# Two-way stage: the next batch's rows turned between two convolution products, and a batch's outputs behind the third

## The reference, cut to what matters

```python
residual = x
xn = layer_norm(x, ln_g, ln_b)
proj = xn @ Wi + bi
xg, z = (proj[..., :D], proj[..., D:])
f = conv1d_same(xg, Wf_conv, bf_conv)
f = simple_ssm(f, af, bf, cf, df)
b_in = jnp.flip(xg, axis=1)
bb_out = conv1d_same(b_in, Wb_conv, bb_conv)
bb_out = simple_ssm(bb_out, ab, bb, cb, db)
bb_out = jnp.flip(bb_out, axis=1)
zg = jax.nn.silu(z)
y = f * zg + bb_out * zg
return y @ Wo + bo + residual
```

## Time and profile before

| | us |
|---|---|
| median of 3 runs | 2517.73 (2516.26 to 2517.88) |
| the profiled execution, its own time | 2510.39 |
| its span, first to last instruction | 2508.4 |
| two-way stage, from GpSimd's first clearing of `xA` to the last addition of outputs | 1757.70 to 1939.76 |
| TensorE busy in the span | 2218.3 (88%) |
| VectorE busy in the span | 1376.1 (55%) |
| ScalarE busy in the span | 1142.9 (46%) |
| GpSimd busy in the span | 879.5 (35%) |
| mean granted TensorE clock, 1 is full speed | 0.948 |

### The profile page before, as it was taken

How to read it: one execution, slowest core, us unless ns; L and a number is a source line. 1 busy time by engine, 2 the same in 40 slices (tenths; PEclk the granted TensorE clock), 3 DMA queues, 4 the chain that set the end, 5 groups by cost and what they waited for, 6 DMA issues and landing times. The chain is left out here.

```text
span 2508.4 us, 45795 instructions
## 1 busy us (share of the span) xinstructions
PE 2218.3 (88%) x16643; PEld 2035.3 (81%) x16643; DVE 1376.1 (55%) x3656; ACT 1142.9 (46%) x2203; POOL 879.5 (35%) x769
## 2 busy tenths in 40 slices
PE   2999999999999999999999885949697889978988
PEld 1999999899899899899899885949355566668988
DVE  4666667567567567567567552412576355532222
ACT  1655665555555555555555441312333455533320
POOL 4445555554554554554554531111321000000000
PEclk9999999999999999999999897979899899988989
DMA  5600000000000000000000202555000010108966
GB/s 167 214 4 4 4 4 5 7 6 4 7 5 4 9 4 4 9 4 4 9 4 2 62 1 76 175 168 157 19 14 5 25 50 38 50 37 274 330 215 220
DMA packets 101337, 150.66 MB, mean 60 GB/s; under 512 B 14692, under 2 KB 79118, under 8 KB 100364
## 3 DMA queue, kind: packets, MB, share of 16 engines
q1 hardware_dynamic: 77580, 118.36, 14.9%
q10 hardware_dynamic: 17984, 20.30, 2.5%
q0 software_dynamic: 5568, 9.27, 1.2%
HBM read 102.32 MB, written 45.50 MB: 59 GB/s over the span
## 5 line engine op out<-in xcount | busy, mean ns | idle before, releaser
L292 PE MATMUL banks<-t_wt,t_l 128*128 128x128 f32 x8508 | 1058.2, 279 | 4.1 <-ACT t_l L369 2.9
L292 PEld LDWEIGHTS banks<-t_wt,t_l 128*128 128x128 f32 x8508 | 1027.6, 195 | 18.9 <-ACT t_l L369 3.7
L468 POOL TENSOR_TENSOR t_rstd<-t_var,t_minus_half 128x4 f32<-128x4 f32 (+1 forms) x379 | 367.0, 968 | 690.6 <-DVE t_var L397 690.4
L351 ACT ACTIVATE t_sq<-banks 128x512 f32<-128x512 f32 (+1 forms) x379 | 216.0, 570 | 530.9 <-PE banks L292 529.3
L405 DVE TENSOR_TENSOR t_yn<-banks,t_rstd 128x512 f32<-128x512 f32 (+1 forms) x379 | 249.2, 657 | 348.3 <-POOL t_rstd L468 341.9
L385 ACT ACTIVATE t_l<-banks,t_cols 128x512 f32<-128x512 f32 x376 | 286.8, 778 | 121.1 <-PE banks L341 117.7
L394 DVE TENSOR_REDUCE t_ss<-t_sq 128x4 f32<-128x512 f32 (+1 forms) x379 | 245.3, 647 | 151.2 <-ACT t_sq L351 142.3
L474 POOL TENSOR_TENSOR t_zrstd<-t_zvar,t_minus_half 128x8 f32<-128x8 f32 x188 | 307.7, 1637 | 25.4 <-DVE t_zvar L432 25.4
L369 ACT ACTIVATE t_l<-banks,t_cols 128x512 f32<-128x512 f32 (+1 forms) x381 | 285.1, 748 | 16.5 <-PE banks L301 11.7
L301 PE MATMUL banks<-t_ident,t_yn 128*128 128x128 f32 x1426 | 219.4, 273 | 17.1 <-DVE t_yn L405 15.8
L301 PEld LDWEIGHTS banks<-t_ident,t_yn 128*128 128x128 f32 x1426 | 172.6, 142 | 32.4 <-DVE t_yn L405 20.2
(11 more groups left out here) (331 smaller groups left out, 3354.7 us busy)
## 6 DMA issues: line engine op xcount, KB each, us to landing
t_w<-in_w SPq DMA_DIRECT2D x64, 480.0 KB
t_w<-in_w SPq DMA_DIRECT2D x27, 576.0 KB, 5.3
ect<-t_ECT SPq DMA_DIRECT2D x16, 750.0 KB, 3.2
t_l<-in_w1a SPq DMA_DIRECT2D x27, 384.0 KB, 3.8
sorted_by_expert<-t_h SPq DMA_DIRECT2D x4, 2400.0 KB, 11.0
routed_by_expert<-t_h SPq DMA_DIRECT2D x4, 2400.0 KB, 17.5
t_ectb<-ect ACTq DMA_DIRECT2D x5, 1500.0 KB, 7.9
t_w1x<-in_w1x SPq DMA_DIRECT2D x64, 97.5 KB
```

The source lines that it names most:

```text
L292: mm = pe.matmul(psY[bank][:, t * C:(t + 1) * C], src[:, at:at + P], T["wt"][:, 3 * (layer - 1) + k, :], start=(k == 0), stop=(k == 2))
L351: act.activation(T["sq"][:, par, 0:n], psY[bank][:, 0:n], ACT.Square).then_inc(S["squared"], 1)
L468: pool.tensor_tensor(T["rstd"][:, par, 0:n], T["var"][:, par, 0:n], T["minus_half"][:, 0:n], ALU.pow)\
```

## The change

Three things are moved and one wait is added.

1. TensorE: the turning becomes a function of its own, `turn(b)`, taken out of `inputs(b)`. turn(b+1) now stands between the second and the third product of batch b. outputs(b-1) stands behind the third product of batch b, where it stood between the second and the third.
2. ScalarE: reading the turned rows becomes `read_turned(b)`. That of batch b+1 stands ahead of the reads of batch b's third product.
3. VectorE: the addition of outputs becomes `add_out`. In the round of batch b it adds the outputs of batch b-1, behind norm(b+2); those of the last batch follow after the loop. The semaphore `two_out` is counted up by the last addition itself and no longer by an empty instruction behind it.
4. Waits: turn(b) waits for `two_out` of b-2 (b at least 3), which stands for the addition of batch b-3's outputs. outputs(b) waits besides until ScalarE has read the turned rows of batch b+2, which lie in the bank that it writes.

```diff
+            def turn(b):
+                pe.wait_ge(S["xh_ready"], b + 1)
+                if b >= 3:
+                    pe.wait_ge(S["two_out"], b - 2)
+                turn_tiles(pe, T, xh, 0, pA, pB).then_inc(S["xh_turned"], 1)
+
             def inputs(b):
-                pe.wait_ge(S["xh_ready"], b + 1)
-                if b >= 2:
-                    pe.wait_ge(S["two_out"], b - 1)
-                turn_tiles(pe, T, xh, 0, pA, pB).then_inc(S["xh_turned"], 1)
                 pe.wait_ge(S["n_ready"], 2 * (b + 1))
...
             def outputs(b):
                 pe.wait_ge(S["y2_ready"], b + 1)
+                if b + 2 < B:
+                    pe.wait_ge(S["n_ready"], 2 * (b + 3))
                 if b >= 1:
                     pe.wait_ge(S["two_out"], b)
...
-            inputs(0)
-            for m in range(3):
-                conv(0, m)
-            for b in range(1, B):
+            turn(0)
+            for b in range(B):
                 inputs(b)
                 conv(b, 0)
                 conv(b, 1)
-                outputs(b - 1)
+                if b + 1 < B:
+                    turn(b + 1)
                 conv(b, 2)
+                if b >= 1:
+                    outputs(b - 1)
             outputs(B - 1)
...
                 for m in range(3):
+                    if m == 2 and b + 1 < B:
+                        read_turned(b + 1)
                     act.wait_ge(S["conv2_done"], 3 * b + m + 1)
...
+            def add_out(b):
+                dve.wait_ge(S["two_done"], b + 1)
+                for t in range(TPB):
+                    n = min(TOK, LEN - t * TOK)
+                    ins = dve.tensor_tensor(htile(T, b, t)[0:n], htile(T, b, t)[0:n],
+                                            pO[t // 2][0:n, (t % 2) * D:(t % 2 + 1) * D], ALU.add)
+                ins.then_inc(S["two_out"], 1)
...
                 if b + 2 < B:
                     norm(b + 2)
-                dve.wait_ge(S["two_done"], b + 1)
-                for t in range(TPB):
-                    n = min(TOK, LEN - t * TOK)
-                    ins = dve.tensor_tensor(htile(T, b, t)[0:n], htile(T, b, t)[0:n],
-                                            pO[t // 2][0:n, (t % 2) * D:(t % 2 + 1) * D], ALU.add)
-                link(ins)
-                dve.nop().then_inc(S["two_out"], 1)
+                if b >= 1:
+                    add_out(b - 1)
+            add_out(B - 1)
```

More of the change, by code:

```diff
@@ L1693, in _, with read_turned @@
             act.wait_ge(S["pads_zero"], 1)
-            for b in range(B):
+            def read_turned(b):
                 act.wait_ge(S["xh_turned"], b + 1)
@@ L1701, in _ @@
                                scale=T["lncol"][:, 1:2]).then_inc(S["n_ready"], 1)
+            read_turned(0)
+            for b in range(B):
                 if b >= 1:
@@ L1767, in _ @@
             for b in range(B):
-                link = Link(dve, S["two_link"], 10, b)
+                link = Link(dve, S["two_link"], 9, b)
                 s, bu, du = T["scan"], T["bu"], T["du"]
```

## The result

| | us |
|---|---|
| before, median of 11 runs | 2514.24 (2509.85 to 2517.88) |
| changed, median of 11 runs | 2522.92 (2519.16 to 2527.22) |
| ratio, with its 95% interval | 1.0035 (1.0026 to 1.0044) |
| changed, the profiled execution and its span | 2525.37, 2523.6 |

The change makes the kernel 8.7 us slower; 7.65 us were forecast. (Over 11 runs the kernel before has a median 3.5 us under that of the first three, on which the forecast of 2525.4 was put; the sum was about the difference.) The two profiled executions are 15.0 us apart. Part of that isn't the change: the first turning starts at 1773.14 before and at 1778.06 now, in code that is the same. From the first turning to the end of the last addition it is 1939.76 - 1773.14 = 166.62 us before and 1953.69 + 0.88 - 1778.06 = 176.51 now.

The account below looks back on a forecast made before the run. The stage looked bound by TensorE's queue plus the exposed reading; after the change, by a loop through VectorE's chain and addition. +5.95 us without the clock plus 1.7 for one clock fall gave +7.65, forecast 2525.4 us, range 2520 to 2533.

Parts of the forecast that it names:

- third product of batch 0 later by the turning: Stage start: turn(1) finds its rows done and runs ahead of batch 0's third product, which ends 0.65 us later.
- turning 2, released by the rows alone, without the clock: Batch 2's turning waits for scaled rows but no addition: a round of 19.45 us, adding 0.12.
- five rounds through the addition: Turnings 3 to 7 wait for VectorE's addition of outputs: five rounds of 20.37 us, each +1.04, together +5.20.
- last batch, TensorE goes through: The last batch's round has no turning, so TensorE takes 16.75 us instead of 19.33: -2.58.
- last outputs behind the addition: Stage tail: outputs(7) wait for the addition of batch 6's outputs and start at 1937.56 instead of 1935.00: +2.56.
- sum without the clock: Whole stage: lag of 3.39 us at the last third product plus 2.56 in the tail, +5.95 us.
- low clock: TensorE behind the 3.89 us gap before turning 2: one 3.4 us fall to 1.2 GHz, +1.7 us; bounds 0 and 10.2.
- chain of seven terms: Round from third product to third product: 15.49 + 0.03 + 0.89 + 0.06 + 0.11 + 0.65 + 3.14 = 20.37 us.
- The cover: ScalarE's reading of turned rows (1.88 us) lies under the third product (3.14); the outputs' added wait costs nothing.
- The intended gain: Rival: scaled rows are there when the second product ends, so reading is hidden and nothing late; -9.9 us, 2507.8; 6%.
- That the addition isn't in the loop: Rival: scaled rows alone release the turnings, each round 19.45 us; +1.35, 2519.1, no measurable change; 12%.
- A fall of the clock at every turning: Rival: TensorE's clock falls six times at 1.7 us each, on top of 5.95; +16.2, 2533.9; 10%.

Follow-up runs that it names:

- filler: Changed kernel plus useless matmuls ahead of turnings from batch 2 on (6 for batch 2, 4 for others), filling TensorE's gap; 2516.83 us, ratio 1.0016 against the kernel before.
- turn_behind_third: Against the kernel before: turning stays behind the third product, previous batch's outputs follow it, only the last output tile waits for bank 1; 2499.41 us, ratio 0.9944.

## Why the prediction was right

The forecast was +7.65 us, slower; measured +8.7 (by the ratio, +6.5 to +11.1). By its steps, the measured side from the changed kernel's profile:

| step | predicted | measured |
|---|---|---|
| third product of batch 0 later by the turning | +0.65 | (1799.00 - 1778.06) - (1793.38 - 1773.14) = +0.70 |
| turning 2, released by the rows alone, without the clock | +0.12 | 19.39 - 19.33 = +0.06 (filler) |
| five rounds through the addition | 5 x 1.04 = +5.20 | 5 x 0.91 = +4.55 |
| last batch, TensorE goes through | -2.58 | 16.65 - 19.33 = -2.68 |
| last outputs behind the addition | +2.56 | (1949.55 - 1940.62) - (1935.00 - 1928.72) = +2.65 |
| sum without the clock | +5.95 | +5.28 |
| low clock | +1.7 | 2.83 + 1.55 + 0.27 = +4.65 |
| sum | +7.65 | +9.93, against 9.89 from the positions |

That the total came this near is in part luck. The sum without the clock was 0.67 us too high and the clock 2.95 too low in this execution, so two errors of opposite sign stand in it.

**The loop.** The chain of seven terms came out at 20.24 instead of 20.37 us, and that it sets the round is shown from both sides: taking the addition out gave 19.40 (forecast for a release by the rows: 19.45), and putting an instruction of 0.76 us into it gave 0.67 more. The 0.13 us too many are in the joints. The addition starts 0.09 us inside the scaled rows' length where I had put a step of 0.03 behind it (-0.12); its release takes 0.14 instead of 0.06 (+0.08); and the turning with the extra of its first matmul takes 0.67 instead of 0.76 (-0.09), since the 0.11 us that I took from a pair of products is less for a small transpose.

**The cover.** Where I costed the reading and the added wait at nothing, that held: behind batch 0 the inputs start without a wait everywhere, and so do the outputs but for the last, which wait for the addition as forecast. VectorE's wait for the addition (0.90) is gone, and in its place the one before the last scans is longer: 3.11 us in an undisturbed round, 2.9 forecast, and up to 5.8 us in the rounds with the low clock.

**The clock.** This is the term that was mis-sized. I took one fall of 3.4 us at 1.2 GHz, behind the gap before turning 2, for 1.7. Both the number of falls and the length of the first were wrong. The granted clock stood at 0.50 from 1813.75 to 1820.33, 6.6 us of which TensorE worked in 5.8, and that cost 2.83; and it fell a second time, from 1837.40 to 1840.80, 3.4 us with 3.2 of work, behind a gap of 2.75 us, for 1.55. The length isn't the same from one execution to the next: behind the same gap of 3.8 us before turning 2 the round was 22.22 and 22.12 us in two kernels' profiles and 20.86 in two others', so the 4.65 is this execution's and not the median's. The last 0.27 is the last outputs, of which more ran at the low clock behind 6.82 us of idle than behind 6.12. With the filling matmuls the slowdown is 5.3 us smaller by the medians, each of the two slowdowns known to about 2.4 us, so the clock is about half of it, and no closer than that. The spread of the runs doesn't show it: 8.1 us for the changed kernel and 8.0 for the one before.

**The rivals.** The intended gain is there in the trace, the whole 13.8 us of it less the first 1.4, and is lost again behind VectorE. Where TensorE's bubble is removed without a new one, as in turn_behind_third, it pays. The prediction drew on a page for this rival (the Trainium skill, Perfetto Trace Analysis, Identifying the Most-Contended Engine) and read it wrongly: judged by its weight loads, as that section asks, TensorE is busy for 11.23 us of the round and VectorE for 14.74, so in this stage the section points at VectorE. That agrees with the trace, in which VectorE's chain releases five turnings, but the busy time alone doesn't tell which chain the moved step will wait for. That the addition isn't in the loop is refuted by its release of five turnings and by the rounds of 19.4 us once it is out. A fall of the clock at every turning didn't come in the changed kernel, but it did with 0.7 us more of gap.

## What to carry to other kernels

When work is moved earlier in one engine's queue, add up the closed chain through the other engines before counting the gap that it fills: here the turning had 3.84 us of slack at its old place, was reached 5.7 us sooner (13.61 instead of 19.33 us into the loop: the third product and the turning with its reading no longer stand ahead of it), and took everything queued behind it along. A wait on a shared buffer puts the step that frees it into that chain, and where such a step is not on the way (an addition of old outputs), another engine's wait can hide it. A stall put in front of the work that closes the loop can cost twice: in the rounds where TensorE came out of it at the lower clock (two of six here, all six with one instruction more), the turning and the product behind it took 5.3 to 6.8 us instead of 3.8, and the loop had no slack for that.

## What was not expected of the hardware

How steeply the cost rises with the gap was not expected. In these kernels the granted clock stayed at 1.00 behind all gaps of 1.87 us or so before turnings (ten of them, in two kernels); fell behind one of five gaps of 2.75; behind all five of 3.43; and behind all four of 3.8 (the turning of batch 2 in the four kernels without filling). One VectorE instruction of 0.76 us in the loop lengthened a round by 0.67 us with TensorE kept busy and by 3.6 us without, and the time by 15 us. (The 15 us are 23.7 - 8.7, two differences that were measured apart.) At gaps of that size a small delay is not a small cost. What lets the clock fall behind one gap of 2.75 us and not behind four others of the same length, these runs don't show.
